# Two attention layers with routed experts: layer 1's scores are exponentiated before they are bounded, and the first unit's preparation is reordered

## The chip, the cores and the metric

The kernel runs on one core of a Trainium2 chip. The core has TensorE (PE, matmuls; PEld in the profile is its weight loading), VectorE (DVE), ScalarE (ACT), GpSimd (POOL) and SyncE (SP, which here only issues DMAs). Each runs its own list of instructions in order; they meet through semaphores. The metric is the time of one execution on the device in microseconds.

## What is computed

A two-layer network on x (8 batches of 256 tokens, 256 wide) and a context of 256 tokens, 192 wide, for each batch:

```python
x = x + tanh(g_xattn[0]) * L0_xattn(layernorm(x), ctx, ...)
x = x + tanh(g_ffn[0])   * L0_ffn(layernorm(x), ...)     # 8 small experts and a shared one, each run on all tokens
x = x + tanh(g_xattn[1]) * L1_xattn(layernorm(x), ctx, ...)
x = x + tanh(g_ffn[1])   * L1_ffn(layernorm(x), ...)     # 8 experts of width 1024, 2 for each token
```

Both attentions have 16 heads of width 16. Layer 1 differs in the lines that matter here:

```python
attn = jnp.einsum('bhqd,bhkd->bhqk', q, k) * scale
attn = jnp.clip(attn, -CLAMP, CLAMP)                     # CLAMP = 10000
attn = jax.nn.softmax(attn, axis=-1)
attn = jnp.where(jnp.any(jnp.isnan(attn)), 1.0 / Nkv, attn)
```

Layer 0 has no clip.

## The kernel before

The attention is cut into 16 **units** (8 batches of layer 0, then 8 of layer 1), each of 8 **pairs** of heads. A **slot** is one step in which every engine deals with about one pair. The scores of a pair are computed twice on PE. `scores_by_query` writes `by_query`, and DVE takes each query's maximum from it (`maxima`). Once all 8 pairs of a unit are through, DVE turns the maxima into rows to subtract (`shifts`), PE transposes them, ACT copies them to `shiftT` (`shift_turn`), and SP sends `shiftT` to DRAM and from there into two more rows of the stacked queries (`place_shift`). Ten slots (LAG) after the first product, `scores_by_key` writes `by_key` with the maximum already subtracted, ACT takes the exponential of 128x1024 into `probs` (`exponentials`), and three slots later PE multiplies two pairs of `probs` with the values (`weigh_values`).

`by_key` has one buffer. In layer 0 ACT reads it and so frees it. In layer 1 DVE reads it: `clip` (L1268) takes min(score, 0) and the maximum with a lower bound for each head and query (-CLAMP less the row's maximum), in two instructions of 128x512, into `clipped`; ACT's exponential (L1057) reads `clipped`. PE's next `scores_by_key` waits for the clip. The bounds come to all partitions by a DMA of 256 KB for each pair (`load_lower`, L515), into one of two `lower` buffers, issued by SP once the clip of two pairs earlier is done.

Beside the pairs, `make_plan` spreads all other work by a table in half slots, relative to each unit's base: the context's transposition (`ctx`), the keys' product (`kprod`), the norm (`stats` on DVE and POOL, `normal` on ACT), its transposition (`turn`), the queries' product (`qprod`), the stacks' loads (`stack`: after keys and queries have been stored to DRAM in a high and a low part, SP loads 12 pieces of 128 KB), the values (`vprod`), the attention's end (`take`, `turn_values`, `attn_turn`, `project`), and the small experts of layer 0, whose work lies from unit 1 to about the fourth unit of layer 1. On PE and DVE a slot is in this order: first the product or maximum of `by_query`, then the table's stages, then `by_key` or its clip. On ACT the exponential is last in its slot. SP goes through its stages in the same order and stops at every semaphore that isn't there yet.

At the start SP loads the gates, x, the context, the weights and the bias columns; DVE fills ones, waits for all eight loads of weights, and scales wq by 1/4; PE waits for the last constant of POOL. The large experts (L915, L931) begin when attention is over, at about 792 us.

## Time and profile before

| | us |
|---|---|
| runs | 1073.37, 1077.26, 1077.18 (median 1077.18) |
| the profiled execution | 1083.7 |
| its span, first to last instruction | 1081.9 |
| PE busy | 943.0 (87%) |
| DVE busy | 757.0 (70%) |
| ACT busy | 479.5 (44%) |
| POOL busy | 222.6 (21%) |

The profiled execution is 6.5 us longer than the median of the others. A busy PE isn't the same as a full one: the granted clock has two levels, 2.4 GHz (written 1.00) and 1.2 GHz (0.50), and a stretch between them has had both. Times that follow are microseconds from the start of the span.

### The profile page before, as it was taken

Reading aid. Unit: us, or ns where it says so; the run is one execution under the profiler, and the core shown is the slowest. Engines: PE = TensorE matmul, PEld = TensorE weight load, DVE = VectorE, ACT = ScalarE, POOL = GpSimd, SP = SyncE. Lnnn points to the kernel's source line nnn. Section 1 sums busy time; section 2 is a strip of 40 time slices with the busy share of each in tenths; the row PEclk is TensorE's granted clock in tenths of the full one; section 3 lists DMA queues with packets and bytes.
Section 4 is the critical chain, followed back from the end, with each engine's and each line's share of the span. In section 5 each row is a group of like instructions: output and inputs, shape, how many; then the busy total and the mean of one; then the engine's idle time right before and its main releaser. Section 6 shows DMA issues by size and latency. Waiting matters only on the chain.

```text
span 1081.9 us, 17951 instructions
## 1 busy us (share of the span) xinstructions
PE 943.0 (87%) x6385; PEld 745.0 (69%) x6385; DVE 757.0 (70%) x1553; ACT 479.5 (44%) x834; POOL 222.6 (21%) x386
## 2 busy tenths in 40 slices
PE   3478899999999998899888868897479999999995
PEld 2345677777777665666655545564379999999995
DVE  2544475777676667788786688865668888888882
ACT  1115544344444442333423343442256667666762
POOL 2011210120201000000000012201044454445423
PEclk9756899999999998999989776655579999999998
DMA  4997563353262316366353873241257677667752
GB/s 117 203 224 151 108 124 61 52 106 69 50 100 54 62 61 110 87 109 139 83 108 94 157 202 96 87 122 42 108 197 243 197 231 235 217 202 233 236 152 29
DMA packets 121336, 142.16 MB, mean 131 GB/s; under 512 B 11456, under 2 KB 105560, under 8 KB 121120
## 3 DMA queue, kind: packets, MB, share of 16 engines
q1 hardware_dynamic: 112416, 128.77, 47.5%
q0 software_dynamic: 8832, 12.25, 5.2%
q8 instruction: 51, 0.84, 0.3%
q14 instruction: 37, 0.30, 0.1%
HBM read 109.97 MB, written 31.01 MB: 130 GB/s over the span
## 4 chain that ended last, share of the span: by engine, by line
PE 62%; DVE 20%; issue 7%; ACT 5%; DMA 3%; POOL 2%; SPq 1%; DVEq 0%; POOLq 0%; ACTq 0%
PE bank L931 12%; PE bank L770 7%; PE by_query L915 6%; PE by_key L915 6%; DVE rowmax L1243 5%; PE value_bank L714 4%; PE bank L780 4%; DVE clipped L1268 4%; PE bank L741 3%; PE by_query L678 3%; PE bank L634 3%; PE bank L625 3%; PE by_key L699 2%; PE bank L664 2%; DVE x L1398 1%
## 5 line engine op out<-in xcount | busy, mean ns | idle before, releaser
L1243 DVE TENSOR_REDUCE rowmax<-by_query 128x4 f32<-128x1024 f32 x128 | 155.7, 1217 | 26.6 <-PE by_query L678 26.4
L1057 ACT ACTIVATE probs<-clipped 128x1024 f32<-128x1024 f32 x64 | 67.6, 1057 | 183.7 <-DVE clipped L1268 183.7
L1702 POOL TENSOR_SCALAR rstd<-moments 128x2 f32<-128x2 f32 x32 | 7.1, 223 | 579.5 <-DVE moments L1207 579.5
L1753 POOL DMA_INDIRECT out_x<-x,token_i x46 | 78.2, 1700 | 146.5 <-ACT x L1158 139.5
L931 PE MATMUL bank<-w_hi,h_hi 128*128 128x256 f32 x368 | 104.1, 283 | 0.0
L931 PE MATMUL bank<-w_lo,h_hi 128*128 128x256 f32 x368 | 104.1, 283 | 0.0
L931 PE MATMUL bank<-w_hi,h_lo 128*128 128x256 f32 x368 | 104.1, 283 | 0.0
L678 PE MATMUL by_query<-stack_k,stack_q 48*128 48x256 f32 x512 | 70.9, 358 | 28.7 <-DVE rowmax L1243 23.2
L1268 DVE SCALAR_TENSOR_TENSOR clipped<-by_key,lower 128x512 f32<-128x512 f32 x128 | 82.0, 682 | 13.2 <-DMA lower<-max 11.1
L678 PEld LDWEIGHTS by_query<-stack_k,stack_q 48*128 48x128 f32 x512 | 43.2, 208 | 68.3 <-issue 35.5
L699 PE MATMUL by_key<-stack_q,stack_k 50*128 50x256 f32 x512 | 68.1, 348 | 19.6 <-DVE clipped L1268 15.6
L770 PE MATMUL bank<-xnT,w_gate 128*128 128x256 f32 x288 | 79.5, 399 | 5.5 <-DVE lo L1224 2.2
L780 PE MATMUL bank<-w_down,hidden 128*128 128x256 f32 x288 | 79.2, 398 | 4.6 <-DVE hidden L1384 1.5
L714 PE MATMUL value_bank<-probs,values 128*32 128x256 f32 x1024 | 80.4, 439 | 0.0
L699 PEld LDWEIGHTS by_key<-stack_q,stack_k 50*128 50x128 f32 x512 | 43.7, 209 | 48.3 <-issue 23.3
L770 PE MATMUL bank<-xnT,w_up 128*128 128x256 f32 x288 | 75.7, 386 | 0.0
L1398 DVE SCALAR_TENSOR_TENSOR x<-bank,expert_cols,x 128x256 f32<-128x256 f32 x144 | 62.5, 476 | 17.9 <-PE bank L780 17.8
L1090 ACT ACTIVATE act_gate<-bank 128x256 f32<-128x256 f32 x72 | 27.4, 380 | 103.8 <-PE bank L770 103.8
L1057 ACT ACTIVATE probs<-by_key 128x1024 f32<-128x1024 f32 x64 | 65.4, 1022 | 16.8 <-PE by_key L699 15.3
L931 PEld LDWEIGHTS bank<-w_hi,h_hi 128*128 128x128 f32 x368 | 70.7, 192 | 0.0
L931 PEld LDWEIGHTS bank<-w_lo,h_hi 128*128 128x128 f32 x368 | 70.7, 192 | 0.0
L931 PEld LDWEIGHTS bank<-w_hi,h_lo 128*128 128x128 f32 x368 | 70.7, 192 | 0.0
(230 smaller groups left out, 2215.7 us busy)
## 6 DMA issues: line engine op xcount, KB each, us to landing
w<-in_L_ffn_W SPq DMA_DIRECT2D x46, 1024.0 KB, 8.8
lower<-max SPq DMA_DIRECT2D x64, 256.0 KB, 3.5
stack_k<-qk SPq DMA_DIRECT2D x96, 128.0 KB, 4.7
stack_q<-qk SPq DMA_DIRECT2D x96, 128.0 KB, 7.2
qk<-hi SPq DMA_DIRECT2D x32, 256.0 KB, 3.5
qk<-lo SPq DMA_DIRECT2D x32, 256.0 KB, 4.3
rows<-w_gate SPq DMA_DIRECT2D x8, 264.0 KB, 3.8
x<-in_x SPq DMA_DIRECT2D x8, 256.0 KB, 6.9
```

The costliest lines, as they stand in the source:

```text
L678: mm = pe.matmul(by_query[:, side, t * S:t * S + S], sq[rows, p, t * P:t * P + P], sk[rows, p, :], start=True, stop=True)
L699: mm = pe.matmul(by_key[:, side, kt * S:kt * S + S], sk[rows, p, kt * P:kt * P + P], sq[rows, p, :], start=True, stop=True)
L714: mm = pe.matmul(value_bank[32 * c:32 * c + 32, o:o + S], values[u % 2][:, kt, 4 * j + c, :], probs[(i + c // 2) % 4][:, c % 2, kt, :], st ...
L770: mm = pe.matmul(bank[:, half * S:half * S + S], w[:, k, e, :], turned_of(("ffn0", b))[:, k, :], start=k == 0, stop=k == 1)
L780: mm = pe.matmul(bank[:, t * D:t * D + D], hidden0[i % 6][:, t * P:t * P + P], w_down0[:, e, :], start=True, stop=True)
L915: mm = pe.matmul(up_bank[pair][:, half * SLOTS:half * SLOTS + SLOTS], wt[:, k, j * P:j * P + P], xt[:, k, :], start=n == 0, stop=n == len( ...
L931: mm = pe.matmul(bank[:, t * D:t * D + D], ht[:, j, t * P:t * P + P], wt[:, j, :], start=j == 0 and t == 0 and n == 0, stop=j == JH - 1 an ...
L1057: ac.activation(probs[i % 4][:, :, :, :].rearrange("p h k s -> p (h k s)"), src, ACT.Exp).then_inc(sem.exp_done, 1)
L1243: dv.tensor_reduce(rowmax[u % 2][:, 2 * p:2 * p + 2, :], by_query[:, :, :].rearrange("p h (t s) -> p h t s", t=TT), AX, ALU.max).then_inc( ...
L1268: op = dv.scalar_tensor_tensor(clipped[i % 2][:, side, :, :], by_key[:, side, :].rearrange("p (k s) -> p k s", k=2), 0.0, lower[j % 2][:, ...
L1398: op = dv.scalar_tensor_tensor(xt, bank[:, t * D:t * D + D], expert_cols[b % 2][:, t, e:e + 1], xt, ALU.mult, ALU.add)
L1753: po.indirect_dma_start(out[:, :], bass.IndirectOffsetOnAxis(ap=token_i[:, n:n + 1].bitcast(U32), axis=0), ysb[i % 3][:, t, :], None, comp ...
```

## The change

**Layer 1.** ACT takes the exponential straight from `by_key`, as in layer 0, and DVE then bounds the exponential in place: min with 1 and max with exp(bound), one instruction of 128x1024 for a pair, with all operands in SBUF. `clipped` is gone. The clip stands one slot later in DVE's order than before, PE's `scores_by_key` waits for the exponential of the pair ahead, and `weigh_values` waits for the clip. `shift_turn` has one more small exponential (for the bounds) ahead of its copy. SP issues each load of `lower` after the clip of two pairs earlier, as before, and that clip is now a slot later; a unit's second `lower` is loaded a slot later than `place_shift` instead of in it.

**First unit.** The preparation of unit 0 is written out as `FIRST`, the norm ahead of the keys' product; scaling wq becomes a stage of its own; the queries are stored to DRAM by ACT; keys' and queries' stacks are two stages. The gates' and the bias columns' loads go to ACT's queue, wkv's first half ahead of wq on SP's. PE waits for the identity alone. The fill of `values` moves behind the fills of the other stacks. In layer 0 the stored block of shifts has 64 rows instead of 96.

```diff
+FIRST = [("stats", ("query", 0)), ("ctx", 0), ("normal", ("query", 0)), ("scale_queries", 0), ("turn", ("query", 0)),
+         ("kprod", 0), ("stack_keys", 0), ("qprod", 0), ("stack_queries", 0)]
...
+        if u == 0:
+            for i, stage in enumerate(FIRST):
+                at[g - 30 + i].append(stage)
+        else:
+            at[g - 28].append(("ctx", u))
...
+            at[g - 10].append(("stack_keys", u))
+            at[g - 10].append(("stack_queries", u))
...
+    at[2 * base(NB) - 40].append(("scale_queries", 1))
...
         def store_queries(u):
             l, b = layer_of(u), batch_of(u)
+            if u == 0:
+                return
             sp.wait_ge(sem.q_hi, u + 1)
...
         def place_shift(u):
             l, b = layer_of(u), batch_of(u)
             sp.wait_ge(sem.shiftT_ready, u + 1)
-            sp.dma_start(max_dram[l][b], shiftT[:, :]).then_inc(sem.shift_out, 16)
+            rows = 3 * H * TT if l else 2 * H * TT
+            sp.dma_start(max_dram[l][b, 0:rows], shiftT[0:rows, :]).then_inc(sem.shift_out, 16)
...
             if l:
                 load_lower(u, 0)
-                load_lower(u, 1)
...
-        sp.dma_start(g_raw[:, 0:2], a["g_xattn"].partition_broadcast(P)).then_inc(sem.gates_in, 16)
-        sp.dma_start(g_raw[:, 2:4], a["g_ffn"].partition_broadcast(P)).then_inc(sem.gates_in, 16)
         load_x(0)
         load_ctx(0)
...
             u, p = divmod(g - base(0) - LAG, PAIRS)
-            if NB <= u < UNITS and 1 <= p < PAIRS - 1:
+            if NB <= u < UNITS and p < PAIRS - 1:
                 load_lower(u, p + 1)
...
         def scores_by_key(u, p):
...
-            if i > PAIRS * NB:
-                pe.wait_ge(sem.clip_done, i - PAIRS * NB)
-            elif i:
+            if i:
                 pe.wait_ge(sem.exp_done, i)
...
         def weigh_values(u, j):
...
-            pe.wait_ge(sem.exp_done, i + 2)
+            if layer_of(u):
+                pe.wait_ge(sem.clip_done, i - PAIRS * NB + 2)
+            else:
+                pe.wait_ge(sem.exp_done, i + 2)
...
-                                   probs[(i + c // 2) % 4][:, c % 2, kt, :], start=kt == 0, stop=kt == 1)
+                                   probs[(i + c // 2) % 4][:, kt, c % 2, :], start=kt == 0, stop=kt == 1)
...
-        pe.wait_ge(sem.const, 1)
+        pe.wait_ge(sem.ident_ready, 2)
...
         def qprod(u):
...
+            if u == 0:
+                ac.wait_ge(sem.q_hi, 1)
+                ac.dma_start(qk_dram[0][0, 0].rearrange("(k p) s -> p k s", p=P),
+                             split[1][0][:, :, :].bitcast(F32)).then_inc(sem.q_out, 16)
+                ac.wait_ge(sem.q_lo, 1)
+                ac.dma_start(qk_dram[0][0, 1].rearrange("(k p) s -> p k s", p=P),
+                             split[1][1][:, :, :].bitcast(F32)).then_inc(sem.q_out, 16)
...
         def shift_turn(u):
...
-            ac.activation(shiftT[:, :], banks[BANK_OF["shift_turn", u][0]][0:3 * H * TT, 0:P], ACT.Copy).then_inc(
-                sem.shiftT_ready, 1)
+            if layer_of(u):
+                ac.activation(shiftT[bounds, :], bank[bounds, 0:P], ACT.Exp)
+            ac.activation(shiftT[0:2 * H * TT, :], bank[0:2 * H * TT, 0:P], ACT.Copy).then_inc(sem.shiftT_ready, 1)
...
         def exponentials(u, p):
...
-            if layer_of(u):
-                ac.wait_ge(sem.clip_done, i - PAIRS * NB + 1)
-                src = clipped[i % 2][:, :, :, :].rearrange("p h k s -> p (h k s)")
-            else:
-                ac.wait_ge(sem.qk2_done, i + 1)
-                src = by_key[:, :, :].rearrange("p h s -> p (h s)")
-            ac.activation(probs[i % 4][:, :, :, :].rearrange("p h k s -> p (h k s)"), src, ACT.Exp).then_inc(
-                sem.exp_done, 1)
+            ac.wait_ge(sem.qk2_done, i + 1)
+            ac.activation(probs[i % 4][:, :, :, :].rearrange("p k h s -> p h k s"),
+                          by_key[:, :, :].rearrange("p h (k s) -> p h k s", k=2), ACT.Exp).then_inc(sem.exp_done, 1)
...
+        for dst, col in ((qkb[0][:, 0, :], a["L0_xattn_q_b"]), (qkb[0][:, 1, :], a["L0_xattn_kv_b"][0:D]),
+                         (vb[0][:, :], a["L0_xattn_kv_b"][D:2 * D])):
+            ac.dma_start(dst, col.rearrange("(k p) -> p k", p=P), allow_slow_non_contiguous=True).then_inc(attn_w_in[0], 16)
+        ac.dma_start(g_raw[:, 0:2], a["g_xattn"].partition_broadcast(P)).then_inc(sem.gates_in, 16)
+        ac.dma_start(g_raw[:, 2:4], a["g_ffn"].partition_broadcast(P)).then_inc(sem.gates_in, 16)
         ac.wait_ge(sem.gates_in, 32)
         ac.activation(tg[:, :], g_raw[:, :], ACT.Tanh).then_inc(sem.gates_ready, 1)
-        ac.wait_ge(attn_w_in[0], ATTN_W)
...
         def clip(u, p):
...
             dv.wait_ge(lower_in[j % 2], 16 * (j // 2 + 1))
-            if j >= 2:
-                dv.wait_ge(sem.exp_done, i - 1)
-            dv.wait_ge(sem.qk2_done, i + 1)
-            for side in range(2):
-                op = dv.scalar_tensor_tensor(clipped[i % 2][:, side, :, :],
-                                             by_key[:, side, :].rearrange("p (k s) -> p k s", k=2), 0.0,
-                                             lower[j % 2][:, side:side + 1, :].broadcast_to([P, 2, S]), ALU.min, ALU.max)
-            op.then_inc(sem.clip_done, 1)
+            dv.wait_ge(sem.exp_done, i + 1)
+            bound = lower[j % 2][:, :, :].rearrange("p h s -> p (h s)").unsqueeze(1).broadcast_to([P, 2, 2 * S])
+            dv.scalar_tensor_tensor(prob, prob, 1.0, bound, ALU.min, ALU.max).then_inc(sem.clip_done, 1)
...
+        def scale_queries(l):
+            dv.wait_ge(attn_w_in[l], ATTN_W)
+            dv.tensor_scalar(qkb[l][:, 0, :], qkb[l][:, 0, :], QSCALE, None, ALU.mult)
+            dv.tensor_scalar(wq[l][:, :, :], wq[l][:, :, :], QSCALE, None, ALU.mult).then_inc(sem.wq_ready, 1)
...
-            u, p = divmod(g - base(0) - LAG, PAIRS)
+            u, p = divmod(g - base(0) - LAG - 1, PAIRS)
             if NB <= u < UNITS:
                 clip(u, p)
```

In the start, SP's list is this before, from the first context's store to unit 1's keys (hi and lo are the two parts of queries or keys, L464/L467 keys, L473/L476 queries):

```order
L437 DMA ctx_t<-ctxT 96x2x256
L464 DMA qk<-hi 128x2x256
L467 DMA qk<-lo 128x2x256
L386 DMA x<-in_x 128x2x256
L391 DMA ctx_tok<-in_ctx 128x2x192
L473 DMA qk<-hi 128x2x256
L476 DMA qk<-lo 128x2x256
L437 DMA ctx_t<-ctxT 96x2x256
L489 DMA stack_k<-qk 16x8x256 x6
L495 DMA stack_q<-qk 16x8x256 x6
L464 DMA qk<-hi 128x2x256
L467 DMA qk<-lo 128x2x256
```

and this now (keys are L474/L477):

```order
L447 DMA ctx_t<-ctxT 96x2x256
L474 DMA qk<-hi 128x2x256
L477 DMA qk<-lo 128x2x256
L501 DMA stack_k<-qk 16x8x256 x6
L512 DMA stack_q<-qk 16x8x256 x6
L395 DMA x<-in_x 128x2x256
L400 DMA ctx_tok<-in_ctx 128x2x192
L447 DMA ctx_t<-ctxT 96x2x256
L474 DMA qk<-hi 128x2x256
L477 DMA qk<-lo 128x2x256
```

The stacks' loads stand ahead of the loads of x and context and of unit 1's work, and the queries' two stores have left the list. They are on ACT, in its list of the first unit, from the context's copy on:

```order
L975 ACTIVATE ctxT,ctx_sum<-bank 96x256 x2
L1043 ACTIVATE xn<-x,rstd 128x256 x2
L1060 ACTIVATE xnT<-bank 128x512
L985 ACTIVATE hi<-bank,qkb 128x256 x2
L995 ACTIVATE hi<-bank,qkb 128x256 x2
L1000 DMA qk<-hi 128x2x256
L1003 DMA qk<-lo 128x2x256
L975 ACTIVATE ctxT,ctx_sum<-bank 96x256 x2
```

On PE the start was this (L609 context, L625 keys' product, L655 the norm's transposition, L664 queries' product):

```order
L609 MATMUL bank<-ident,ctx_tok 96x128 x4
L625 MATMUL bank<-ctxT,wkv 128x256 x4
L655 MATMUL bank<-ident,xn 128x128 x4
L664 MATMUL bank<-xnT,wq 128x256 x4
L609 MATMUL bank<-ident,ctx_tok 96x128 x4
```

and is this:

```order
L624 MATMUL bank<-ident,ctx_tok 96x128 x4
L670 MATMUL bank<-ident,xn 128x128 x4
L640 MATMUL bank<-ctxT,wkv 128x256 x4
L679 MATMUL bank<-xnT,wq 128x256 x4
L624 MATMUL bank<-ident,ctx_tok 96x128 x4
```

The norm's transposition now stands ahead of the keys' product.

On DVE, at the first two pairs of layer 1's `by_key` (L1243 maxima, L1268 clip, L1398 adds an expert's result to x, L1380/L1384 an expert's hidden values), before:

```order
L1243 TENSOR_REDUCE rowmax<-by_query 128x4
L1398 SCALAR_TENSOR_TENSOR x<-bank,expert_cols,x 128x256 x2
L1268 SCALAR_TENSOR_TENSOR clipped<-by_key,lower 128x512 x2
L1380 SCALAR_TENSOR_TENSOR act_t<-act_gate,bank 128x256
L1384 TENSOR_TENSOR hidden_2<-act_t,bank 128x256
L1243 TENSOR_REDUCE rowmax<-by_query 128x4
L1398 SCALAR_TENSOR_TENSOR x<-bank,expert_cols,x 128x256 x2
L1268 SCALAR_TENSOR_TENSOR clipped<-by_key,lower 128x512 x2
```

and now (L1267, L1292, L1419, L1401/L1405 in that order):

```order
L1267 TENSOR_REDUCE rowmax<-by_query 128x4
L1419 SCALAR_TENSOR_TENSOR x<-bank,expert_cols,x 128x256 x2
L1401 SCALAR_TENSOR_TENSOR act_t<-act_gate,bank 128x256
L1405 TENSOR_TENSOR hidden_2<-act_t,bank 128x256
L1267 TENSOR_REDUCE rowmax<-by_query 128x4
L1419 SCALAR_TENSOR_TENSOR x<-bank,expert_cols,x 128x256 x2
L1292 SCALAR_TENSOR_TENSOR probs<-probs,lower 128x1024
```

The first clip has moved behind the next slot's maximum, and is one instruction.

On SP, from unit 8's `place_shift` on (the first of layer 1; L500 stores the shifts, L505 puts them in the stack, L515 loads `lower`), before:

```order
L500 DMA max<-shiftT 96x128
L505 DMA stack_q<-max 2x8x256 x2
L515 DMA lower<-max 128x512 x2
L473 DMA qk<-hi 128x2x256
L476 DMA qk<-lo 128x2x256
L515 DMA lower<-max 128x512 x2
L489 DMA stack_k<-qk 16x8x256 x6
L495 DMA stack_q<-qk 16x8x256 x6
L515 DMA lower<-max 128x512
```

and now (L518, L523, L532):

```order
L518 DMA max<-shiftT 96x128
L523 DMA stack_q<-max 2x8x256 x2
L532 DMA lower<-max 128x512
L485 DMA qk<-hi 128x2x256
L488 DMA qk<-lo 128x2x256
L532 DMA lower<-max 128x512 x3
L501 DMA stack_k<-qk 16x8x256 x6
L512 DMA stack_q<-qk 16x8x256 x6
L532 DMA lower<-max 128x512
```

The second `lower` of the unit has moved behind the queries' stores. The three `lower` loads of the unit ahead, which stand before the next `place_shift`, are the same, but each waits for a clip that stands a slot later on DVE.

## Rows read from the trace of the kernel before

**Rows 1.** Windows: busy us (instructions) per engine, then PE clock, DMA share, GB/s.
```profile
0.00:45.00 45.00, 13.25 (x40) 9.18 (x40) 16.50 (x24) 8.93 (x22) 8.56 (x39) 0.89 0.62 130
45.00:82.00 37.00, 26.25 (x95) 18.60 (x97) 17.83 (x26) 6.07 (x16) 3.33 (x9) 0.59 1.00 245
...
190.00:396.00 206.00, 203.43 (x1326) 149.21 (x1326) 147.24 (x372) 87.54 (x162) 23.91 (x76) 1.00 0.39 70
396.00:596.00 200.00, 175.20 (x1083) 124.31 (x1081) 153.76 (x356) 68.61 (x135) 12.67 (x48) 0.97 0.47 101
596.00:745.00 149.00, 124.13 (x769) 80.18 (x769) 109.89 (x280) 58.95 (x95) 26.39 (x71) 0.68 0.50 126
```
**Rows 2.** Timeline of the start: start us, length us, engine, line, operation, idle before.
```profile
11.31 0.17 DVE L1555 TENSOR_SCALAR qkb<-qkb 128x2 f32<-128x2 f32 x1 [6.03 <-DMA vb<-in_L_xattn_kv_b]
12.29 3.75 PE L625 MATMUL bank<-ctxT,wkv 96*128 96x256 f32 x8 [4.35 <-ACT ctxT L959]
17.82 0.75 DVE L1203 BATCH_NORM_STATS2 stats<-x 128x6 f32<-128x256 f32 x2
...
24.71 3.75 PE L664 MATMUL bank<-xnT,wq 128*128 128x256 f32 x8 [0.78 <-ACT xnT L1037]
30.27 0.37 SPq L476 DMA_DIRECT2D qk<-lo  x1
31.29 2.78 SPq L489 DMA_DIRECT2D stack_k<-qk  x6
...
42.20 1.76 DVE L1550 MEMSET stack_k<- 32x2048 f32 x1 [0.47 <-issue]
45.08 0.80 PE L678 MATMUL by_query<-stack_k,stack_q 48*128 48x256 f32 x4 [4.94 <-DMA stack_q<-qk]
```
**Rows 3.** Timeline of PE: first by_key product of units 4, 8 and 12.
```profile
223.29 0.50 PE L699 MATMUL by_key<-stack_q,stack_k 50*128 50x256 f32 x4
...
394.91 0.51 PE L699 MATMUL by_key<-stack_q,stack_k 50*128 50x256 f32 x4
...
595.39 0.50 PE L699 MATMUL by_key<-stack_q,stack_k 50*128 50x256 f32 x4 [0.50 <-DVE clipped L1268]
```
**Rows 4.** PE's waits from 396 to 596: waiter, releaser, us, times, longest.
```profile
PE by_key L699 <- DVE clipped L1268: 6.5, 7, 1.9
PE bank L741 <- ACT attnT L1071: 3.2, 3, 1.2
```
**Rows 5.** PE's waits from 596 to 745.
```profile
PE by_key L699 <- DVE clipped L1268: 9.2, 11, 2.1
PE bank L724 <- ACT weighted L1064: 5.1, 6, 1.2
PE by_query L678 <- DVE rowmax L1243: 5.0, 6, 2.0
```
**Rows 6.** Groups by line: xcount, busy us, mean ns, idle before and releaser.
```profile
L1268 DVE SCALAR_TENSOR_TENSOR clipped<-by_key,lower 128x512 f32<-128x512 f32 x128 | 82.0, 682 | 13.2 <-DMA lower<-max 11.1
L1057 ACT ACTIVATE probs<-by_key 128x1024 f32<-128x1024 f32 x64 | 65.4, 1022 | 16.8 <-PE by_key L699 15.3
L1630 DVE TENSOR_TENSOR h_lo<-x,h_hi 128x512 fp32r<-128x512 f32 x92 | 63.8, 693 | 3.2
L1600 DVE TENSOR_TENSOR w_lo<-w,w_hi 128x2048 fp32r<-128x2048 f32 x23 | 52.7, 2292 | 15.5 <-ACT w_hi L1123 15.3 <-issue 0.3
```
**Rows 7.** Timelines of SP, DVE and PE around the shifts of units 9 and 13.
```profile
437.03 0.33 SPq L500 DMA_DIRECT2D max<-shiftT  x1
440.56 1.28 DVE L1268 SCALAR_TENSOR_TENSOR clipped<-by_key,lower 128x512 f32<-128x512 f32 x2
446.46 0.40 PE L699 MATMUL by_key<-stack_q,stack_k 50*128 50x256 f32 x4
...
625.73 0.34 SPq L500 DMA_DIRECT2D max<-shiftT  x1
632.87 0.80 PE L699 MATMUL by_key<-stack_q,stack_k 50*128 50x256 f32 x4 [0.94 <-DMA stack_q<-max]
```

57 lines of the change are left out of this document (27 added, 30 removed).

## The prediction

> **What bounds the kernel now.** I read the windows first [rows 1]. From 190 to 396 us PE is busy 203.4 of 206 us at clock 1.00: layer 0 with the small experts beside it is bound by PE. From 396 to 596 the same kind of work, now with layer 1's clip, leaves PE idle for 24.8 of 200 us, while DVE is busy 153.8. From 596 to 745, without the small experts, PE is idle 24.9 of 149 us, at a clock of 0.68, and DVE is busy 109.9. In the start, up to 45 us, PE works 13 us. The pace tells the same [rows 3]: four units took 394.91 - 223.29 = 171.6 us in layer 0, 42.9 each, and 200.5 us in layer 1, 50.1 each.
>
> Then the waits [rows 4, 5]. What ends PE's waits in layer 1 most often is the clip, which holds `by_key`: 6.5 us and 9.2 us. Behind it stand others that come from the same loop: ACT is in order and its exponential waits for the clip, so `attnT` (3.2 us) and `weighted` (5.1 us), behind it in ACT's list, come late too. The rest is spread over DVE's other results, such as `rowmax` (5.0 us). The loop is: by_key's product, clip, next by_key's product; and DVE reaches the clip only after the maximum and the experts' work of its slot.
>
> **The start.** Before, the first product of scores stands at 45.08, held by the queries' stack for 4.94 us [rows 2]. Back from there: stack loads from 31.29, the queries' low part stored at 30.27, the queries' product at 24.71, at whose head lies the norm, which began at 17.82. Norm to product is 24.71 - 17.82 = 6.9 us. Now the norm begins when x is there. No row shows x landing; the fills of DVE and the first load end by about 6 us at the earliest and the last weights came at 11.31, which bounds it. I take 6 to 7, the time at which DVE was free before (11.31 less its 6.03 us idle, 5.3) and a little more. The norm and its transposition then end PE's part at about 12 to 13, the keys' product (3.75 us) follows at about where it was (12.29), the queries' product behind it at 16 to 17, ending at 20 to 21. Before, from that product's start to the store of the low part were 30.27 - 24.71 = 5.6 us, so now 21.5 to 22.5. That is 8 to 9 us earlier. The stacks' loads took 45.08 - 31.29 = 13.8 us for all twelve; the keys' six can now start ahead of the queries' store, at about 22. Both ways the last lands at about 36. DVE must also be through: its fills ended at 42.20 + 1.76 = 44.0, and they now follow the second unit's norm, which comes earlier by the same 8 to 9 us, plus the fill of `values` (1 us, by the other fills' size at most 1.8). So the first maximum is at about 37 and the gain 8 to 9 us. From 45 to 82 us the DMA engines' share is 1.00 [rows 1]: the experts' weights are loaded there, and SP's later stores stand behind their issue. Part of the head start can be lost in that. I take **-8 us**, bounds -3 and -10.
>
> Putting stores and columns on ACT's queue could seem to give a second path. The windows show the 16 engines full from 45 on. The Trainium skill, "DMA: Bandwidth & Descriptors", section "Issuing engines are not separate DMA queues", says that transfers run on the same engines whoever issues them and that only issuing time is saved; by it the change earns only places in SP's list, and the term stays at -8. Were ACT's queue a path of its own, the term would lie at its bound, -10.
>
> **Layer 1, 396 to 596.** Removed: PE's wait for the clip (6.5 us) and, through ACT, `attnT` (3.2). The exponential from `by_key` takes 1.02 us [rows 6], shorter than the pair of clips, 1.28 us at 440.56 [rows 7], and it begins when the product ends, since ACT is busy only 68.6 of 200 us [rows 1]. The clip: the trace has no two-tensor instruction of 128x1024 from SBUF to SBUF. By 693 ns for 512 and 2292 for 2048 [rows 6], which is 1.04 ns an element and 160 ns fixed, it would take 1.23 us, against 1.28 before: 0.05 us less for each of 64, 3 us of DVE in all. Two instructions of 512 in its place would be 1.39, 7 us more in all; without the fixed part it would be 1.07, 13 us less in all. I take 1.23, since two sizes of its own kind give it.
>
> What comes late next is DVE. It does 153.8 us in this stretch, less 1.6; if PE became as full as in layer 0 (98.8%), the stretch would be about 177 us and DVE busy 86%, and it is in order and waits for ACT's results in between. The maximum of a slot must be done before PE's next slot, so a slot with much on DVE still holds PE. So the ceiling is 24.8 - 2.1 = 22.7 us, the floor the waits that are named, 6.5 with little to follow. I take **-14 us**, rather more than half of the ceiling, since 9.7 is named and part of the other waits hangs on the same loop. The unit goes from 50.1 to 46.6 us.
>
> **Layer 1, 596 to 745.** Named: 9.2 + 5.1 = 14.3 us. DVE waits 11.1 us for `lower` [rows 6], mostly here; the clip comes a slot later after the shifts, which gives a unit's first bound more time. Against it: more waits for `rowmax`, with DVE busy 110 of then fewer us (I take 2), and the shifts, next. I take **-10 us**, bounds -3 and -25 (all of its idle time).
>
> **The moved waits on SP.** `place_shift` stands behind a load of `lower` that waits for the clip of pair 5 of the unit before, now a slot later. In unit 9 the store of the shifts was issued at 437.03, and the clip at 440.56, a slot after the one waited for, ends at 441.8: up to 4.8 us later, if DVE kept its pace. The by_key product that needs them came 9.4 us after the store; in unit 13 it came 7.1 us after it, held by the DMA [rows 7]. So unit 9 had 9.4 - 7.1 = 2.3 us of slack. But DVE now takes the late clip without waiting for that slot's product, so I put the delay at 2 us, between 0 and 4.8: hidden in the first four units, and in the last three, without slack, 2 us each, of which the bounds' gain of a slot gives back a part. Taken: 2 us; 14.3 - 2 - 2 is the 10 above. The lone exponential of the bounds is 32x128; ACT has room for it (0.3 us on a path of 7), at nothing. The 64 instead of 96 rows, the moved scaling of wq and PE's earlier release by the identity change no other term.
>
> From 745 on nothing is changed; it moves ahead as a whole.
>
> **The sum.** -8 - 14 - 10 = -32 us against the profiled execution, 1083.7, is 1051.7. That execution was 6.5 us above the median of the runs, so against the median, 1077.2, it is **1045 us**.
>
> **The rivals.**
>
> *PE's clock comes back.* In 596 to 745 the clock was 0.68, and PE's busy time is long for that reason; in 190 to 396, where PE was full, it was 1.00 [rows 1]. If fewer gaps keep it at the upper level, DVE with 110 us and some waits bounds the stretch, at about 125 us: -24 instead of -10. With the stretch ahead at -17, the sum is -49, 1028 us. The Trainium skill, "TensorE: Matmul & The Clock Gate", section "HAM oscillation — how this bites in real kernels", says that idle gaps bring the clock down; the row at 0.68 with 17% idle agrees. Against it: that stretch has less work for PE, and the gaps from `rowmax` stay. Chance 0.15.
>
> *The wait only changes its name.* DVE's in-order list is the true limit of layer 1: PE waits for `rowmax` and the experts' hidden values in place of the clip. For it: DVE's 77% with waits in between. Against: the same waits cost PE nothing in layer 0. Then layer 1 gives 8 and the start 8: 1061 us. Chance 0.16.
>
> *SP holds the shifts.* If the late clip delays `place_shift` by a full slot of 6.3 us (50.1/8) at each of seven units, beyond its slack, PE stands still in its in-order list each time, and the clock falls with it. Price: 7 x 6.3 = 44 us; 1045 + 44 = 1089 us, slower. It decides from 37/7 = 5.3 us for each unit beyond the slack. Against it: unit 9's slack. Chance 0.05.
>
> *The change doesn't do what it says.* Should the exponential from `by_key` stand behind other waits of ACT, the product would be held as long as now, and only the start is left: 1069 us. ACT's idle time speaks against it. Chance 0.04.
>
> **How the numbers follow.** The forecast has 0.60, between 1035 (-8 - 18 - 16) and 1057 (-6 - 9 - 5), terms halfway to their bounds. The range from 1022 to 1065 takes in the clock's rival, the changed name, and the bounds of the terms (-3 - 6.5 - 3 = -12.5 gives 1065); left out are the last two rivals and the tails, 0.13 or so. About 0.5% (5.4 us) is what a measurement of this kernel can tell from no change. Faster: 0.60 + 0.15 + 0.16 and 0.01 of the last rival, 0.92; same 0.03; slower 0.05.
>
> **What would show it.** The first `by_query` product at 36 to 38 us. The in-place bound at 1.2 us. No wait of PE for the clip at `by_key`; in 396 to 596, as shifted, PE over 92% busy; the last by_key product 28 to 36 us earlier. `by_key` of units 9 to 15 waiting for the shifts' DMA by 2 us or less. I am wrong if PE's idle time stays near 25 us in either stretch under other names, or if the shifts' wait is 5 us for each unit.

## The result and the profile after

| | before | after |
|---|---|---|
| median of the runs, us | 1075.6 (1071.1 to 1077.3) | 1065.7 (1064.1 to 1069.8) |
| ratio | | 0.9921, interval 0.9897 to 0.9944 |
| profiled execution, us | 1083.7 | 1065.4 |

The change made the kernel 8 to 10 us faster, by the ratio and by the medians. I had forecast 1045 us with a range up to 1065: the sign was right, the size not. The two profiles differ by 18.3 us, since the profiled execution of before was 8 us over its median; a second one, below, took 1079.6.

The windows of the changed kernel, with columns as in [rows 1] and the stretches of layer 1 moved with its first and fifth unit (units 8 and 12):

```profile
0.00:45.00 45.00, 19.24 (x70) 14.23 (x72) 21.64 (x31) 10.50 (x28) 8.62 (x39) 0.84 0.83 189
...
190.00:383.00 193.00, 190.75 (x1245) 140.09 (x1245) 134.79 (x337) 82.04 (x153) 20.58 (x67) 1.00 0.36 68
383.00:574.00 191.00, 172.30 (x1086) 125.42 (x1086) 154.30 (x326) 74.25 (x140) 16.02 (x49) 0.96 0.49 105
574.00:727.00 153.00, 114.45 (x773) 75.09 (x773) 108.50 (x248) 60.02 (x98) 35.04 (x71) 0.71 0.51 124
```

In the first stretch of layer 1 PE is idle for 18.7 of 191 us (before 24.8 of 200, on a window a little later). In the second it is idle for 38.6 of 153 us, where it was 24.9 of 149 [rows 1]: more gaps, not fewer, though the clip no longer holds `by_key`. These windows don't end at the same product. Over the same products, from the first `by_key` of unit 8 to the last of unit 15, before and then changed:

```profile
394.90:736.80 341.90, 293.37 (x1810) 201.19 (x1809) 261.64 (x626) 124.69 (x225) 38.01 (x115) 0.85 0.49 114
```
```profile
382.90:715.00 332.10, 279.67 (x1812) 196.58 (x1811) 256.34 (x556) 131.63 (x233) 47.78 (x112) 0.86 0.51 114
```

Layer 1 is nearly 10 us shorter, but PE's idle time rose from 48.5 to 52.4 us. All of the gain lies in PE's busy time, 13.7 us less for the same products, at nearly the same mean clock. It goes with layer 1's edit, since the two kernels below with one part each have 293.8 us (start alone) and 281.2 us (layer 1 alone) there. Why the products got shorter, no run shows.

The timeline of PE at units 4, 8 and 12 [rows 3]:

```profile
211.31 0.50 PE L712 MATMUL by_key<-stack_q,stack_k 50*128 50x256 f32 x4
...
382.91 0.50 PE L712 MATMUL by_key<-stack_q,stack_k 50*128 50x256 f32 x4
...
573.95 0.80 PE L712 MATMUL by_key<-stack_q,stack_k 50*128 50x256 f32 x4 [3.54 <-DMA stack_q<-max]
```

Four units of layer 1 went from 200.5 to 191.0 us, 47.8 each; the forecast had 46.6. The row of unit 12 names what holds it now. So do PE's waits, first from 383 to 574, then from 574 to 727 (waiter, releaser, us, times, longest):

```profile
PE by_key L712 <- DMA stack_q<-max: 11.8, 4, 3.5
```
```profile
PE by_key L712 <- DMA stack_q<-max: 16.9, 4, 6.2
PE by_query L693 <- DMA stack_q<-qk: 6.4, 1, 6.4
PE by_query L693 <- DVE rowmax L1267: 4.9, 3, 2.0
PE value_bank L730 <- DVE probs L1292: 4.4, 5, 1.6
```

The clip's 6.5 and 9.2 us of [rows 4, 5] are gone. In their place `by_key` of each unit from 9 on waits for its shifts, and those are the largest wait of both stretches (unit 12's 3.5 us, at the border, is counted in both). The groups of the page (count, busy us, mean ns, idle before and releaser), to be read against [rows 6]:

```profile
L1077 ACT ACTIVATE probs<-by_key 128x1024 f32<-128x1024 f32 x128 | 130.7, 1021 | 66.6 <-PE by_key L712 63.8
L1292 DVE SCALAR_TENSOR_TENSOR probs<-probs,lower 128x1024 f32<-128x1024 f32 x64 | 77.8, 1215 | 14.0 <-DMA lower<-max 10.6
```

The clip costs 1215 ns, as priced (1.23), and DVE still waits 10.6 us for bounds.

The start (timeline) [rows 2]:

```profile
5.31 0.75 DVE L1227 BATCH_NORM_STATS2 stats<-x 128x6 f32<-128x256 f32 x2
...
15.77 2.31 PE L679 MATMUL bank<-xnT,wq 128*128 128x256 f32 x8
19.89 0.40 ACTq L1003 DMA_DIRECT2D qk<-lo  x1
20.02 2.85 SPq L501 DMA_DIRECT2D stack_k<-qk  x6
23.80 2.67 SPq L512 DMA_DIRECT2D stack_q<-qk  x6
34.44 0.80 PE L693 MATMUL by_query<-stack_k,stack_q 48*128 48x256 f32 x4 [3.15 <-DMA stack_q<-qk]
35.27 1.03 DVE L1592 MEMSET values<- 128x512 f32 x2 [0.17 <-issue]
```

The first product of scores came at 34.44, 10.6 us earlier; the first maximum, behind the fill of `values`, at 36.2.

Then the place that the rival on SP had named. SP, ACT, DVE and PE around the shifts of unit 9, and SP and PE for unit 13, as [rows 7]:

```profile
409.92 13.82 SPq L532 DMA_DIRECT2D lower<-max  x3
417.64 0.27 ACT L1070 ACTIVATE shiftT<-bank 64x128 f32<-64x128 f32 x1
422.17 1.22 DVE L1292 SCALAR_TENSOR_TENSOR probs<-probs,lower 128x1024 f32<-128x1024 f32 x1
423.83 0.38 SPq L452 DMA_DIRECT2D ctxT<-ctx_t  x1
424.26 0.45 SPq L518 DMA_DIRECT2D max<-shiftT  x1
427.51 1.23 SPq L523 DMA_DIRECT2D stack_q<-max  x2
430.66 0.79 PE L712 MATMUL by_key<-stack_q,stack_k 50*128 50x256 f32 x4 [2.84 <-DMA stack_q<-max]
...
611.48 0.52 SPq L518 DMA_DIRECT2D max<-shiftT  x1
615.89 1.23 SPq L523 DMA_DIRECT2D stack_q<-max  x2
618.99 0.80 PE L712 MATMUL by_key<-stack_q,stack_k 50*128 50x256 f32 x4 [6.21 <-DMA stack_q<-max]
```

ACT has the shifts ready at 417.9 (the end of the **turn**, as the text calls it from here on). SP stands at the last of three loads of `lower` until the sixth pair's clip ends at 423.4, then issues that load and one of `ctxT`, and the store of the shifts goes at 424.26, 6.4 us after the turn's end; before, the store followed the turn at once (437.03 after a turn that ended at 437.0). The load of the shifts, which waits for the store's landing, goes 3.25 us later still. Over the seven units 9 to 15 the store was 3.1 to 8.6 us late, 45 us in all, and `by_key` waited 25.1 us for the shifts; before, 2.1.

The shifts were not all that stood behind such a load. In unit 12 the twelve loads of unit 14's stacks stood behind three loads of `lower`, of which the last waited for a clip that ended at 586.1:

```profile
586.54 2.73 SPq L501 DMA_DIRECT2D stack_k<-qk  x6
...
602.27 0.80 PE L693 MATMUL by_query<-stack_k,stack_q 48*128 48x256 f32 x4 [6.44 <-DMA stack_q<-qk]
```

They left 12.6 us after unit 12's first `by_key` (before 6.5, at 601.94), and PE waited 6.4 us for them, where before it waited for none in layer 1. They landed at about 602, as did the bounds of unit 12's fifth pair, issued behind them at 593.6; the DMA engines' share was above 1.1 from 592 to 602.

### The profile page after: what moved, and what is told of

The parts are those of the page before. It is cut to its first block, busy times and chain, and to the rows that moved or that the text cites. A ratio compares the mean times of both kernels' runs of the same rounds, so it can differ in the third digit from the quotient of the medians.

```text
span 1063.6 us, 17907 instructions
## 1 busy us (share of the span) xinstructions
PE 922.6 (87%) x6385; PEld 736.5 (69%) x6385; DVE 754.2 (71%) x1489; ACT 486.1 (46%) x842; POOL 235.0 (22%) x386
## 3 DMA queue, kind: packets, MB, share of 16 engines
q1 hardware_dynamic: 110512, 128.11, 48.5%
## 4 chain that ended last, share of the span: by engine, by line
PE 62%; DVE 14%; DMA 10%; SPq 4%; issue 4%; ACT 3%; POOL 2%; ACTq 0%; POOLq 0%; DVEq 0%
PE bank L947 12%; PE bank L786 8%; PE by_key L931 6%; PE by_query L931 6%; PE bank L796 5%; PE value_bank L730 4%; DVE rowmax L1267 3%; PE by_query L693 3%; PE by_key L712 3%; DMA max<-shiftT 3%; PE bank L640 3%; PE bank L757 3%; PE bank L679 2%; DVE probs L1292 2%; PE bank L649 2%
## 5 line engine op out<-in xcount | busy, mean ns | idle before, releaser
L1267 DVE TENSOR_REDUCE rowmax<-by_query 128x4 f32<-128x1024 f32 x128 | 155.5, 1215 | 27.2 <-PE by_query L693 27.0
L1077 ACT ACTIVATE probs<-by_key 128x1024 f32<-128x1024 f32 x128 | 130.7, 1021 | 66.6 <-PE by_key L712 63.8
L1721 POOL TENSOR_SCALAR rstd<-moments 128x2 f32<-128x2 f32 x32 | 9.6, 300 | 545.6 <-DVE moments L1231 545.6
L712 PE MATMUL by_key<-stack_q,stack_k 50*128 50x256 f32 x512 | 66.8, 342 | 29.2 <-DMA stack_q<-max 26.3
L1292 DVE SCALAR_TENSOR_TENSOR probs<-probs,lower 128x1024 f32<-128x1024 f32 x64 | 77.8, 1215 | 14.0 <-DMA lower<-max 10.6
L1419 DVE SCALAR_TENSOR_TENSOR x<-bank,expert_cols,x 128x256 f32<-128x256 f32 x144 | 62.5, 475 | 21.0 <-PE bank L796 20.9
L1649 DVE TENSOR_TENSOR h_lo<-x,h_hi 128x512 fp32r<-128x512 f32 x92 | 63.7, 693 | 3.2
```

Of the source, the lines that this page charges most:

```text
L712: mm = pe.matmul(by_key[:, side, kt * S:kt * S + S], sk[rows, p, kt * P:kt * P + P], sq[rows, p, :], start=True, stop=True)
L1077: ac.activation(probs[i % 4][:, :, :, :].rearrange("p k h s -> p h k s"), by_key[:, :, :].rearrange("p h (k s) -> p h k s", k=2), ACT.Exp) ...
L1267: dv.tensor_reduce(rowmax[u % 2][:, 2 * p:2 * p + 2, :], by_query[:, :, :].rearrange("p h (t s) -> p h t s", t=TT), AX, ALU.max).then_inc( ...
L1292: dv.scalar_tensor_tensor(prob, prob, 1.0, bound, ALU.min, ALU.max).then_inc(sem.clip_done, 1)
L1649: dv.tensor_tensor(hl[:, part, :], relu[pair], hh[:, part, :].bitcast(F32), ALU.subtract).then_inc(sem.h_lo, 1)
```

## The experiments

The theory at this point: the hold of the shifts on SP eats layer 1's gain. The rivals: DVE's list limits layer 1 anyway; all of the gain is the start; the profile of before was untypical. All times after "Measured" are medians, except that of the kernel before once more, which is one execution; a ratio of 0.0010 is 1.1 us. Each trace is of one execution, and some of them were up to 9.5 us below their kernel's median.

**The start alone.** The changed kernel with layer 1's loop as before. In short:

```diff
+                ac.wait_ge(sem.clip_done, i - PAIRS * NB + 1)
+                src = clipped[i % 2][:, :, :, :].rearrange("p h k s -> p (h k s)")
...
+            u, p = divmod(g - base(0) - LAG, PAIRS)
-            u, p = divmod(g - base(0) - LAG - 1, PAIRS)
```

> The changed kernel with layer 1 as it was before: only the start is new (first unit's norm ahead of its keys, stores and small loads on ACT). My theory: the start is worth 7 to 12 us, since the changed kernel's first by_query came 10.6 us earlier and its layer 1 began 12.0 us earlier; layer 1 then runs its old 342 us. Expected ratio to before 0.990 to 0.994, 1065 to 1069 us. The rival that all of the measured 9.9 us is the start, and layer 1 gave nothing, expects the same time as the changed kernel, 1065. The rival that the profiled execution of before (8 us over its median) was untypical at the start expects 3 us or less, 1072 or more.

Measured: 1071.6 us, ratio 0.9955 (0.9931 to 0.9980). That is above the expected 1065 to 1069, next to what the rival of an untypical profile gave (1072 or more). Its first product stood at 33.89 and its layer 1 began at 384.8, but that head start shows as only 4 to 5 us in the medians. The changed kernel's 0.9921 (0.9897 to 0.9944) is lower by 3.7 us, but the intervals overlap a little; the traces part the two: layer 1 took 342.1 us here, as before, and 332.0 in the changed kernel.

**Layer 1 alone.** The changed kernel with the first unit's preparation, stores and loads as before.

```diff
-        if u == 0:
-            for i, stage in enumerate(FIRST):
-                at[g - 30 + i].append(stage)
+        at[g - 28].append(("ctx", u))
+        at[g - 25].append(("kprod", u))
...
```

> The changed kernel with the old start: only the exponential from PSUM and the bounds in place a slot later are new. My theory: 25 us are lost at the shifts, which stand behind the last bounds' load of the unit ahead, and what is left of layer 1's gain is 0 to 4 us on the medians (the traces show 9.9, but 6 to 8 of it may be the profiled execution of before that was above its median): 1072 to 1076 us. If the start is worth 3 or less, this has to be near 1067.

Measured: 1076.0 us, ratio 1.0017 (0.9995 to 1.0038): nothing in the medians. In the whole span its `by_key` waited 28.5 us for the shifts, and in unit 12 the wait for the stacks was there too (6.5 us). Its one trace does show a shorter layer 1, 333.8 us for 341.9, and an end 4.8 us ahead of that of the next run; why the medians show none of it stays open. The two parts alone make -4.8 and +1.8 us, both together -8.5; with intervals of 2 to 3 us each way that is no more than a hint that they help each other.

**The kernel before, once more.**

> The kernel before once more, unaltered, for a second profiled execution, since the first took 1083.7 us against a median of 1075.3. With the first units 4 us slower at a lower clock in the first profile (unit 1 to unit 2 took 31.6 us there and 27.5 in four other traces), I expect this one at 1073 to 1078 us, that period at 27.5, and layer 1 at 342 us again. If layer 1 is the part that differs, the changed kernel gained less there than the two profiles showed.

Measured: 1079.6 us, a single execution, 1.6 us above the expected 1073 to 1078. The period from unit 1 to unit 2 was 27.5 us for 31.6 (from 110 to 140 us PE was busy 27 us in both, with 225 products at a granted clock of 1.00 here and 194 at 0.83 there), and layer 1 began at 390.75 in place of 394.91; from there on the two traces keep the same distance, 4.1 us at the last `by_key`, and layer 1 took 342.0 us again. So 4 us of the difference between the first two profiles was the execution, not the change, and it lay before layer 1. Against this trace the changed kernel's layer 1 began 7.8 us earlier.

**The shifts ahead of the last bounds.** In the changed kernel SP issues the last load of bounds of a unit behind the next unit's shifts; the first lines stand at the end of `place_shift`.

```diff
+            if u > NB:
+                load_lower(u - 1, PAIRS - 1)
             if l:
                 load_lower(u, 0)
...
-            if NB <= u < UNITS and p < PAIRS - 1:
+            if NB <= u < UNITS and (p < PAIRS - 2 or p == PAIRS - 2 and u == UNITS - 1):
```

> The changed kernel with one thing moved on SP's queue: the last load of bounds of a unit is issued behind the shifts of the next unit instead of ahead of them, so that the shifts no longer wait for a late clip. My theory (the shifts are held on SP): by_key's wait for stack_q<-max falls from 26 us to under 8, and layer 1 gets shorter by 10 to 20 us; 1045 to 1055 us. The last pair's bounds then come later, after the shifts, and its clip may wait 1 to 2 us for them, which is why I don't expect the whole 25. The rival that DVE's order limits layer 1 expects the wait to turn up elsewhere (clip, by_query's bank or the matmuls' slower clock), and a time within 3 us of the changed kernel, 1063 to 1069.

Measured: 1056.2 us (1046.6 to 1059.6), ratio 0.9829 (0.9793 to 0.9864), 9.5 us less than the changed kernel and 1 us above what was expected. The trace is that of the fastest execution, 1046.6. Its waits, PE's and DVE's:

```profile
PE by_key L714 <- DMA stack_q<-max: 7.7, 3, 3.9
```
```profile
DVE probs L1294 <- DMA lower<-max: 17.5, 5, 5.8
```

The shifts left 0 to 2.4 us after their turn, and `by_key`'s wait fell as expected (from 26.3 us in the whole span), but the last pairs' bounds came late: DVE's wait rose from 10.6 to 17.5 us. In this trace two buffers are too few for either order.

**Four buffers of bounds.** The order on SP stays; the memory is that of the clipped tiles, which the change had freed.

```diff
-            if j >= 2:
-                sp.wait_ge(sem.clip_done, j - 1)
-            sp.dma_start(lower[j % 2][:, :, :].rearrange("p h s -> p (h s)"),
+            if j >= 4:
+                sp.wait_ge(sem.clip_done, j - 3)
+            sp.dma_start(lower[j % 4][:, :, :].rearrange("p h s -> p (h s)"),
```

> The changed kernel with four buffers of bounds in place of two, in the memory that the clipped tiles gave back: each load of bounds waits for a clip two pairs further back, the order on SP stays. My theory expects the shifts to leave at once when their turn ends on ACT, by_key's wait for them to be 1 us per unit or less, and 1040 to 1052 us, at least as fast as with the load moved behind the shifts, since here no clip waits for its bounds either. If DVE's order is the limit, 1063 to 1069; the DVE waits for lower in the trace would then not have mattered. If the gain is eaten by PE's clock, the idle goes, the granted clock in 574 to 715 stays at 0.73 or falls, and the time is 1055 to 1065.

Measured: 1042.7 us (1040.4 to 1045.1), ratio 0.9692 (0.9661 to 0.9723), 23 to 25 us less than the changed kernel, and faster than both kernels of the case. PE's waits for the shifts in the whole span, and the windows of layer 1:

```profile
PE by_key L712 <- DMA stack_q<-max: 2.6, 2, 2.1
```

```profile
384.00:565.00 181.00, 171.00 (x1085) 124.59 (x1084) 150.97 (x323) 74.13 (x140) 14.99 (x49) 0.97 0.49 113
565.00:700.00 135.00, 112.24 (x750) 73.64 (x749) 109.16 (x243) 60.33 (x97) 35.70 (x71) 0.71 0.53 133
```

DVE had no wait for bounds at all. PE's idle time fell from 18.7 to 10.0 us in the first stretch and from 38.6 to 22.8 in the second, with its clock as in the changed kernel (0.97 for 0.96, 0.71 for 0.71): the gain is idle time, not clock. Over the same products PE was busy for 279.8 us, as in the changed kernel (279.7), and idle for 28.4 instead of 52.4. It waited for no stacks in layer 1 either.

**Four buffers, with the hold put back.** Four buffers give two things, prompt shifts and prompt bounds. This kernel takes the first away again: SP waits for the sixth clip of the unit ahead before the store.

```diff
             sp.wait_ge(sem.shiftT_ready, u + 1)
+            if u > NB:
+                sp.wait_ge(sem.clip_done, PAIRS * (u - NB) - 2)
```

> The changed kernel with four buffers of bounds, and its shifts held by a wait of their own at the point where the changed kernel's two buffers held them: until the sixth pair's clip of the unit ahead. It tells apart the two things that four buffers gave (23 us): shifts that leave at once, and bounds that are there before the clip. My theory: nearly all of it is the shifts, so this takes 1060 to 1066 us, with 20 us or more of waits for stack_q<-max. If it was the clips' waits for their bounds (10.6 us in the changed kernel), 1043 to 1050.

Measured: 1040.3 us, ratio 0.9688 (0.9657 to 0.9719): no loss, where I had expected 1060 to 1066. My theory fell here in its simple form. The trace shows that the hold was there (unit 9, ACT, DVE, SP, PE):

```profile
419.99 0.27 ACT L1072 ACTIVATE shiftT<-bank 64x128 f32<-64x128 f32 x1
...
424.52 1.22 DVE L1294 SCALAR_TENSOR_TENSOR probs<-probs,lower 128x1024 f32<-128x1024 f32 x1
...
425.82 0.33 SPq L520 DMA_DIRECT2D max<-shiftT  x1
...
427.37 1.24 SPq L525 DMA_DIRECT2D stack_q<-max  x2
...
430.62 0.51 PE L714 MATMUL by_key<-stack_q,stack_k 50*128 50x256 f32 x4 [0.44 <-DMA stack_q<-max]
```

The store is 5.6 us late, as in the changed kernel the clip is. But it goes at the clip's end, with nothing issued ahead of it, and the load follows 1.55 us later, not 3.25. PE waits 0.44 us.

**The kernel before, held.** The converse, on the kernel before: the shifts wait for the last clip of the unit ahead.

```diff
             sp.wait_ge(sem.shiftT_ready, u + 1)
+            if u > NB:
+                sp.wait_ge(sem.clip_done, PAIRS * (u - NB))
```

> The kernel before with one wait more: from the second unit of layer 1 on, SP holds the shifts until the clip of the last pair of the unit ahead is done. In the profile of before these clips end 8.6, 8.6, 12.1, 10.4, 6.1, 7.2 and 3.7 us after the shifts' turn, and by_key had 0.4 to 6.6 us to spare (from the turn's end to by_key, less 6.3 us for the two transfers). My theory (a hold of the shifts passes to PE nearly whole): by_key waits some 36 us for stack_q<-max, and the time rises by 20 to 36 us, to 1095 to 1111. The rival (DVE's order limits layer 1, PE's wait only gets another name) expects 0 to 8 us, 1075 to 1083.

Measured: 1108.5 us, ratio 1.032 (1.0277 to 1.0364), 34 us slower, with the store 3.8 to 12.8 us late:

```profile
PE by_key L701 <- DMA stack_q<-max: 34.3, 7, 7.0
```
```profile
DVE clipped L1270 <- DMA lower<-max: 36.0, 9, 5.1
```

A hold of the shifts costs the time, if it is long enough. The first bounds of each unit go out behind them, so the clips came late as well here, and this run alone can't part the two.

**No bounds.** The clip and the loads of bounds are left out (so this kernel doesn't bound the exponentials); what follows waits for the exponential.

```diff
-            if layer_of(u):
-                pe.wait_ge(sem.clip_done, i - PAIRS * NB + 2)
+            pe.wait_ge(sem.exp_done, i + 2)
```

> The changed kernel without the bounding of layer 1's exponentials: no clip on DVE, no loads of bounds on SP, the values' matmuls wait for the exponential alone. It leaves that part of the computation out, and shows what is left to win. My theory: with the shifts free, PE sets the pace; the 18 us that PE still waits for rowmax and for probs in layer 1 with four buffers go, and the clock gives some back: 1020 to 1030 us. The rival (DVE's order limits, the shifts don't matter) expects that 78 us less on DVE show at once, 1015 or less. If PE's clock falls as its waits go, 1035 to 1042.

Measured: 1011.5 us, ratio 0.941 (0.9374 to 0.9445): 31 us less than with four buffers. That is below what my theory gave (1020 to 1030) and inside what the rival gave (1015 or less), though 78 us less on DVE showed as 31, 0.4 us for each. Over the same products of layer 1 as above:

```profile
379.80:659.40 279.60, 266.69 (x1810) 190.44 (x1809) 189.00 (x498) 131.31 (x233) 37.24 (x112) 0.91 0.40 78
```

Against four buffers PE's idle time fell by 15.5 us, to 12.9, and its busy time by 13.1 us, with the clock at 0.91 for 0.87. So about half of what came off is gaps. Gone with the clip are the waits of `value_bank` for it (6.1 us) and the loads of bounds; PE's waits for `rowmax` fell from 26.8 to 22.3 us. DVE's list holds PE in layer 1 too, once the shifts are prompt, but this run doesn't part DVE's time from the rest, and 31 us is the most that the clip's part of it can be worth. The runs with four buffers show that it is not what took the change's gain.

**The last load late.** Four buffers, but the one load ahead of the shifts waits for the sixth clip, as in the changed kernel. It differs from the held kernel in what SP issues right ahead of the store. (The expectation gives that load 512 KB; the page says 256 KB.)

```diff
             if j >= 4:
-                sp.wait_ge(sem.clip_done, j - 3)
+                sp.wait_ge(sem.clip_done, j - 1 if p == PAIRS - 1 else j - 3)
```

> The changed kernel with four buffers of bounds, but the last load of each unit, the one that stands ahead of the shifts on SP, waits for the sixth pair's clip as in the changed kernel. The run before held only the shifts until that clip, 2.6 to 6.4 us after their turn, and lost nothing: its store of the shifts went out at once after the clip and the load of the shifts 1.5 us later (3.1 once). In the changed kernel the store followed the clip's end by 0.5 to 2.9 us and the load of the shifts the store by 2.5 to 4.4 us, with a 512 KB load of bounds issued just ahead. My theory now: by_key had some 5 us per unit to spare, the hold uses that up, and the store's landing behind the bounds' load is what PE waits for; this kernel has both again, so by_key waits 12 to 22 us for stack_q<-max and the time is 1050 to 1060 us. The rival (the clips' own waits for bounds in units 12 and 13, 10 us, were what four buffers won) expects 1039 to 1046.

Measured: 1058.2 us (1056.6 to 1062.5), ratio 0.9842 (0.9812 to 0.9872), 17 us more than the held kernel. SP and PE at unit 9, whose turn ended at 421.4 and the clip at 426.9:

```profile
426.88 0.32 SPq L532 DMA_DIRECT2D lower<-max  x1
...
427.30 0.38 SPq L452 DMA_DIRECT2D ctxT<-ctx_t  x1
427.73 0.45 SPq L518 DMA_DIRECT2D max<-shiftT  x1
...
430.86 1.23 SPq L523 DMA_DIRECT2D stack_q<-max  x2
...
434.20 0.50 PE L712 MATMUL by_key<-stack_q,stack_k 50*128 50x256 f32 x4 [2.91 <-DMA stack_q<-max]
```

Two issues stand between clip and store (0.9 us), and the store takes 3.13 us to land. DVE had no wait for bounds. Everything behind that load on SP is late with it, `ctxT` for one, but of PE's waits from 384 to 760 only that of `by_key` for the shifts grew against the held kernel, from 4.9 to 23.9 us; no other grew by more than 0.2. So the 17 us are the shifts. What is left between this and the changed kernel, 0.9921 - 0.9842 or 8.5 us, goes with DVE's 10.6 us of waits for bounds and with PE's 6.4 us of wait for the stacks, of which this kernel has none in layer 1. No run parts these two.

**Held to the last clip, and to the seventh.** Both are four buffers with a longer hold (`PAIRS * (u - NB)` and `PAIRS * (u - NB) - 1` in the wait above). The second was run last, to test a line drawn through the others.

> The changed kernel with four buffers, and the shifts held until the clip of the last pair of the unit ahead, some 8 us after their turn in place of 5. With 5 us of slack per unit, my theory expects each of the seven units to lose 2 to 5 us: by_key waits of 15 to 30 us for stack_q<-max, 1056 to 1070 us. If the shifts' arrival doesn't set by_key in these kernels (the rival, by which the run with the shorter hold was no slower because they never mattered), 1038 to 1046.

Measured: 1099.6 us, ratio 1.023 (1.0189 to 1.0271), far more than the expected 1056 to 1070: with PE stopped the last clip itself came later still, and the shifts left 13.4 us after their turn, not 8.

> Four buffers, and the shifts held until the seventh pair's clip of the unit ahead, between the holds of two runs before. There the shifts left 5.0 us after their turn on average and nothing was lost (1040.3 us), and 13.4 us after it with 59 us lost in seven units (1099.6): a slack of 13.4 - 59/7 = 5.0 us per unit, if each us beyond it costs one. The last-load run fits (5.8 to 7.7 us late and 1.6 us more to land, 18 us lost, 2.6 per unit). My theory is that line: with the clip of the seventh pair about 9 us after the turn (half way), 4 us per unit and 28 in all are lost, 1068 us, between 1060 and 1076, with by_key waits of 30 us or so for stack_q<-max. The rival is that the loss comes with the order of the last clip on DVE and not with lateness (by_key ahead of or behind it): then the seventh pair costs no more than the sixth, 1038 to 1046.

Measured: 1070.7 us (1064.2 to 1074.9), ratio 0.9957 (0.9929 to 0.9986); expected 1068. `by_key`'s waits for the shifts in the two kernels:

```profile
PE by_key L714 <- DMA stack_q<-max: 63.0, 8, 10.6
```
```profile
PE by_key L714 <- DMA stack_q<-max: 34.9, 8, 6.8
```

**Four buffers and the shifts first.**

> Four buffers of bounds, and the last load of bounds behind the shifts. With four buffers that load waits for a clip that is long done, so the order should be worth nothing more: 1038 to 1045 us, the same as with four buffers alone (1042.7). If the landing of the shifts' store behind a bounds' load still costs something there, it is 2 us per unit faster, 1028 to 1034.

Measured: 1040.7 us, ratio 0.9674 (0.9640 to 0.9708): the same as four buffers alone. With bounds loaded early the order is worth nothing.

The runs with four buffers make a curve. Late is the mean time, over units 9 to 15, from the turn's end on ACT to SP's store of the shifts; landing that from the store to the load of the shifts; both read from the timelines as at unit 9. Loss is the ratio less the held kernel's 0.9688, times 1075.4 us, over 7.

| kernel | late | landing | sum | loss for each unit |
|---|---|---|---|---|
| four buffers | 0.0 | 1.9 | 1.9 | 0.1 |
| held to the sixth clip | 5.0 | 1.8 | 6.8 | 0 |
| last load late | 6.0 | 3.7 | 9.8 | 2.4 |
| held to the seventh clip | 9.5 | 1.6 | 11.1 | 4.1 |
| held to the last clip | 13.4 | 1.6 | 15.0 | 8.3 |

Up to 6.8 us nothing is lost; beyond about 7 us each further us costs one (9.8 - 2.4 = 7.4, 11.1 - 4.1 = 7.0, 15.0 - 8.3 = 6.7). Late and landing are of one execution and the loss is of medians; with the loss from the same executions as the traces (1056.6, 1064.2 and 1093.6 us against 1038.1) the three differences are 7.1, 7.4 and 7.1. The changed kernel stands at 6.4 + 3.6 = 10.0 us, the kernel before at 0 + 3.4.

## Why the prediction was wrong

**The start** was right in its chain, and early by some 2 us: the first product was put at 36 to 38 and came at 34.4, the first maximum at 37 and came at 36.2. Layer 1 began 7.8 us earlier against the second trace of before. In the medians the start alone is worth 4 to 5 us of the 8 forecast; where the rest goes between executions I can't say.

**The clip and the exponential** were right: 1.215 us for 1.23, no wait of PE for the clip at `by_key`. (The prediction says that the trace has no two-tensor instruction of 128x1024 in SBUF. It has one, L1542, with a bf16 result, at 1218 ns.) With prompt shifts and bounds layer 1 gains more than the 24 us that I gave it: from the first `by_key` of unit 8 to the last it took 341.9 us before (394.91 to 736.83), 332.0 in the changed kernel and 308.1 with four buffers. Whole, that is 1042.7 us, and 1040.3 in the held kernel, beside the forecast of 1045. But 8.5 us of that come from bounds and stacks in time, which the change does not bring. Without them the change with free shifts would stand near 1049 (1040.3 + 8.5), an estimate.

Nor is it all the mechanism that I had. All of my 24 us were idle time of PE. With four buffers the idle time fell by 20.1 us; the other 13.6 us are busy time, which only my rival on the clock had, and the mean clock rose merely from 0.85 to 0.87. In the changed kernel itself the idle time rose by 3.9 us, and what layer 1 gained is that other part alone: that the result has the sign I forecast in layer 1 is luck.

**The step that failed is the moved waits on SP.** I put the shifts' delay at 2 us between 0 and 4.8, hidden in the first four units, and charged 2 us to layer 1. Three things were off. The clip that SP waits for ended 2.5 to 6.4 us after the turn, 5.0 on average: the upper bound, 4.8, and not the 2 that I took. My ground, that DVE would take the clip without waiting for that slot's product, overlooked that the clip now stands behind the maximum and the experts' work of the next slot in DVE's order: in these seven units the sixth pair's exponential had been over for 3.6 to 12.9 us when its clip began. Next, I left out what SP issues between that clip and the shifts, one load of bounds and one or more others. In before these went out ahead of the turn; now they stand between clip and store at the moment when time runs, 1.4 us on average, so that the store came 3.1 to 8.6 us after the turn. And the sum of turn to load rose from 3.4 to 10.0 us, of which the slack of 7, as the runs with four buffers have it, covers 3.6. That leaves 3.0 us in each of seven units, 21 us, against 23 us more waits in the trace (25.1 for 2.1) and 17 us between the run with the last load late and the held one. Nor was it hidden in the first four units: `by_key` of units 9 to 12 waited 2.4 to 3.5 us each. My slack was rather too small (2.3 us and none in the last three units); the delay, at 2 for 6.6, was the error. The load of the stacks, with its 6.4 us of PE's time, I hadn't looked for behind the same waits at all. The rival "SP holds the shifts" had the mechanism, with its chance of 0.05 and its full price of 6.3 us per unit both off: 2.4 to 3 us per unit, so its place was inside my own forecast's term, and the case between its price and mine had no chance of its own.

My own mark for being wrong, PE's idle time near 25 us in either stretch under other names, was met: 38.6 us in the second. Of the other marks, PE was busy 90% in the first stretch, not over 92%, the last `by_key` came 21.9 us earlier, not 28 to 36, and the waits for the shifts were 2.4 to 6.2 us for each unit, where 2 was my limit.

**The sum.** Against the first profile the forecast was -32 us (1051.7) and the measured difference -18.3. Of the 13.7 us between them layer 1 is 14.1 (9.9 for 24) and what follows it 3.6, while the start gave 4.0 more than forecast (12.0 for 8, of which 4.2 were that execution's). The 6.5 us by which I then went down to the median of before did not carry over: the changed kernel's profiled execution lay at its own median.

**The other rivals.** The wait did change its name, but to a DMA's, not to `rowmax` (1.3 and 4.9 us); 1061 was near the result for another reason. PE's clock did not come back: 0.68 to 0.71 in the second stretch (0.69 to 0.73 over the same products), and 0.71 also with four buffers. The Trainium skill, "TensorE: Matmul & The Clock Gate", section "HAM oscillation — how this bites in real kernels", has idle gaps bring the clock down; here the share of gaps in that stretch rose from 17% to 25% and the granted clock did not fall. In the first four units of layer 1 some runs do agree with the Trainium skill: with gaps of 6, 10 and 20% (the kernel held to the sixth clip, the changed one, the one held to the last clip) the clock was 1.00, 0.96 and 0.91, and the same products took 166.4, 172.4 and 174.4 us of PE's time. But the kernel before had 12%, 0.97 and 175.8 us, so what gaps cost in clock stays open. The first bound of a unit did get its slot, but DVE's waits for bounds stayed, 10.6 us for 11.1; they were those of the fifth pair in units 12 and 13, 10.2 us, as in the row below, not of the first.

```profile
602.64 1.23 DVE L1292 SCALAR_TENSOR_TENSOR probs<-probs,lower 128x1024 f32<-128x1024 f32 x1 [6.13 <-DMA lower<-max]
```

**After layer 1.** The last `by_key` came 21.9 us earlier, the end only 18.3. I had moved the rest as a whole. What follows the last product waits for the norm of a unit ahead (`rstd`, on POOL), which came only 18.6 us earlier; before, ACT waited 0.6 us for it, at 738.53:

```profile
719.96 1.09 ACT L1043 ACTIVATE w_gate<-x,rstd 128x256 f32<-128x256 f32 x2 [5.06 <-POOL rstd L1728]
```

## What to carry to other kernels

When a producer moves a slot later, list every queue that waits for it only to reuse a buffer, and then what stands behind that wait in the same in-order queue: here a load that nobody was in a hurry for held the store that the next unit needed. Price it as a sum from the event that makes the data ready to the issue of the last transfer, with all that is issued in between, and compare that with the slack: here below it the delay was free, and beyond it each us cost one. Spend memory that an edit frees on the buffers whose waits stand in such a queue; here two more buffers turned 8 to 10 us into 33.
